# Last experts of a two-layer network: six of eight batches routed to tiles of 256 rows of one expert, two left dense

## The chip, the core and the metric

The kernel runs on one core of one Trainium2 chip. The metric is the time of one execution in device microseconds. The core has TensorE (PE, with its weight loads PEld), VectorE (DVE), ScalarE (ACT), GpSimd (POOL) and the queue engine SyncE (SP). Each works through its own list of instructions in order, and they wait for one another through semaphores. Everything is float32.

## The reference

The input is 8 batches of 512 rows of 256 columns. Two layers are computed, each a mixer and a feed-forward part with experts. Only the second layer's feed-forward part matters here; `x` is the running sum of 4096 rows.

```python
flat = layernorm(x)                                  # rows of 256
scores = sigmoid(flat @ Wg.T)                        # 16 experts
s_choice = scores + bias_corr                        # groups of 4: the sum of the two best of each,
                                                     # the 2 best groups, then the 4 best experts in them
w = scores[chosen]; w = w / (sum(w) + 1e-20) * 2.5
hid = relu(einsum('th,eih->eti', flat, W1)) ** 2     # 16 experts, 256 -> 128
y = einsum('eti,ehi->eth', hid, W2)                  # 128 -> 256
out = einsum('eth,te->th', y, cw)                    # cw holds w for the 4 chosen, else 0
shared = relu(flat @ Ws1.T) ** 2 @ Ws2.T             # 256 -> 256 -> 256, every row
x = x + out + shared
```

## The kernel before

Five stages run one after the other: A and B are layer one's mixer and attention, C layer one's experts (routed through DRAM to 35 tiles of 128 rows, with `L1065` scattering rows and `L1827` gathering them on POOL), D layer two's mixer, and E the experts above. Between stages all engines meet. X holds all 4096 rows in the working memory Z (SBUF) throughout, 32 tiles of 128 x 256; PS is PSUM.

Stage E (class `StageE`) computes all 16 experts for all rows. It goes batch by batch. `order` writes one list of steps, and every engine walks that list and does its part of each step:
- `prep(b, p)`, p = 0 to 17: statistics, normalizing, transposing (PE, L2360), logits (PE, L2367), and choosing by comparing each score with each other (DVE, with POOL's multiply and add). Pieces of batch b + 1 stand between the experts of batch b.
- `hidden(b, j)`: two matmuls (each two records in the trace) of 512 columns (L2384), relu on ACT, and the product on DVE (L2517). j = 0, 1 is the shared expert, 2 to 17 the routed ones.
- `down(b, x, i)`: x = 0 is the shared expert, x = 1 to 16 expert x - 1, i the half of the batch. Matmuls of 256 columns (L2402) into one of four PSUM banks, then DVE adds the result times the row's weight `cw` into X (L2532). A bank is taken again when the addition four units back is done (`e.wait_ge(s["acc"], u - 3)`).

SP loads the weights at the stage's start and stores each batch when its 34 `down` units are added.

## Time and profile before

| | us |
|---|---|
| median of three runs | 3163.64 |
| lowest and highest | 3160.22, 3163.8 |
| the profiled execution's own time | 3162.49 |
| its span, first to last instruction | 3160.6 |
| PE busy in the span | 2702.3 (85%) |
| DVE busy | 2132.8 (67%) |
| ACT busy | 1586.8 (50%) |
| POOL busy | 1181.4 (37%) |
| mean granted TensorE clock, full speed is 1 | 0.933 |

Busy times are of the whole span, over five stages with different limits, so what a change in stage E is worth has to be read from that stage. Times inside the trace count from the span's start. A transfer's landing is counted from its issue.

### The profile page before, as it was taken

Reading aid. Unit: us, or ns where it says so; the run is one execution under the profiler, and the core shown is the slowest. Engines: PE = TensorE matmul, PEld = TensorE weight load, DVE = VectorE, ACT = ScalarE, POOL = GpSimd, SP = SyncE. Lnnn points to the kernel's source line nnn. Section 1 sums busy time; section 2 is a strip of 40 time slices with the busy share of each in tenths; the row PEclk is TensorE's granted clock in tenths of the full one; section 3 lists DMA queues with packets and bytes.
Section 4 is the critical chain, followed back from the end, with each engine's and each line's share of the span. In section 5 each row is a group of like instructions: output and inputs, shape, how many; then the busy total and the mean of one; then the engine's idle time right before and its main releaser. Section 6 shows DMA issues by size and latency. Waiting matters only on the chain.

```text
span 3160.6 us, 39455 instructions
## 1 busy us (share of the span) xinstructions
PE 2702.3 (85%) x13080; PEld 1625.4 (51%) x13142; DVE 2132.8 (67%) x4071; ACT 1586.8 (50%) x2357; POOL 1181.4 (37%) x874
## 2 busy tenths in 40 slices
PE   7778878887765689999886999967989988999999
PEld 4445544454443255555544666644444445666666
DVE  1688889788886777877633222227887876777776
ACT  3678778778872245555541111127787781111111
POOL 0788888888882221111101000024455430100000
PEclk9899999899877799999998999988988999999999
DMA  3578878788784765555605000020000002000000
GB/s 114 114 169 148 180 170 161 155 179 168 150 189 96 195 177 102 81 86 87 96 14 188 24 24 22 19 56 7 8 14 7 8 1 61 7 14 7 7 7 14
DMA packets 122343, 262.88 MB, mean 83 GB/s; under 512 B 14785, under 2 KB 76993, under 8 KB 120481
## 3 DMA queue, kind: packets, MB, share of 16 engines
q0 software_dynamic: 28000, 134.89, 20.9%
q1 hardware_dynamic: 94144, 125.47, 17.3%
q8 instruction: 110, 1.80, 0.2%
q14 instruction: 89, 0.72, 0.1%
HBM read 135.40 MB, written 131.20 MB: 84 GB/s over the span
## 4 chain that ended last, share of the span: by engine, by line
PE 47%; DVE 7%; issue 7%; ACT 3%; POOL 2%; DMA 1%; POOLq 0%; DVEq 0%; ACTq 0%
PE PS L2384 7%; PE PS L1676 6%; PE PS L2402 6%; PE PS L1970 3%; PE PS L1698 3%; PE PS L2014 3%; PE PS L1339 2%; PE PS L2032 2%; PE PS L1297 1%; PE PS L1267 1%; PE PS L1321 1%; PE PS L1318 1%; DVE PS L1527 1%; POOL Z L2229 1%; ACT Z L2100 1%
## 5 line engine op out<-in xcount | busy, mean ns | idle before, releaser
L856 POOL TENSOR_TENSOR Z<-Z 128x1024 f32<-128x1024 f32 x256 | 645.2, 2722 | 123.7 <-DVE Z L757 78.6
L764 DVE TENSOR_TENSOR_SCAN Z<-PS,Z 128x1024 f32<-128x1024 f32 x256 | 576.4, 2274 | 20.7 <-ACT PS L684 10.4
L535 PE MATMUL PS<-Z 128*128 128x128 f32 x2048 | 301.4, 293 | 119.9 <-DVE Z L764 48.2
L535 PEld LDWEIGHTS PS<-Z 128*128 128x128 f32 x2048 | 248.3, 150 | 253.0 <-issue 84.1
L684 ACT ACTIVATE PS<-Z 128x511 f32<-128x511 f32 x512 | 332.8, 688 | 65.0 <-DVE Z L764 63.5
L1527 DVE CUSTOM_DVE_ANT_0 PS<-PS,Z 128x512 f32<-128x512 f32 (+3 forms) x512 | 242.2, 511 | 122.5 <-PE PS L1297 117.4
L1435 ACT ACTIVATE Z<-PS 128x512 f32<-128x512 f32 x320 | 188.7, 596 | 254.8 <-PE PS L1321 251.8
L2435 ACT ACTIVATE Z<-PS 128x512 f32<-128x512 f32 x144 | 85.9, 597 | 411.9 <-PE PS L2384 411.9
L696 ACT ACTIVATE Z<-PS,Z 128x512 f32<-128x512 f32 x378 | 245.9, 684 | 77.2 <-PE PS L535 69.1
L2384 PE MATMUL PS<-Z 128*128 128x512 f32 x576 | 273.5, 600 | 7.9 <-DVE Z L2517 7.1
L2100 ACT ACTIVATE Z<-Z 128x2048 f32<-128x2048 f32 x128 | 249.9, 1994 | 34.1 <-PE PS L2014 21.8
L487 PE MATMUL PS<-Z 128*128 128x512 f32 x512 | 246.6, 611 | 9.7 <-ACT Z L604 9.0
L1676 PE MATMUL PS<-Z 128*128 x560 | 248.3, 596 | 0.6 <-issue 0.4
L2402 PE MATMUL PS<-Z 128*128 128x256 f32 x1024 | 243.0, 380 | 1.8 <-DVE Z L2532 1.8
L2402 PEld LDWEIGHTS PS<-Z 128*128 128x128 f32 x1024 | 193.6, 190 | 80.3 <-issue 53.6
L2532 DVE SCALAR_TENSOR_TENSOR Z<-PS,Z 128x256 f32<-128x256 f32 x512 | 213.9, 476 | 9.9 <-PE PS L2402 9.9
L2517 DVE TENSOR_TENSOR Z<-Z,PS 128x512 f32<-128x512 f32 x144 | 98.3, 686 | 130.7 <-ACT Z L2435 130.6
L1574 POOL TENSOR_TENSOR Z<-Z 128x512 f32<-128x512 f32 x32 | 37.0, 1157 | 390.1 <-ACT Z L1400 390.1
L1803 DVE TENSOR_TENSOR Z<-Z,PS 128x512 f32<-128x512 f32 x70 | 48.2, 689 | 197.6 <-PE PS L1676 197.6
L2014 PE MATMUL PS<-Z 128*32 128x512 f32 x1024 | 138.1, 634 | 42.3 <-DVE Z L2201 42.3
L1676 PEld LDWEIGHTS PS<-Z 128*128 128x128 f32 x560 | 104.5, 192 | 119.6 <-issue 119.6
L2201 DVE TENSOR_SCALAR Z<-Z 128x2048 f32<-128x2048 f32 x128 | 157.4, 1242 | 5.6 <-ACT Z L2100 5.2
(293 smaller groups left out, 4896.5 us busy)
## 6 DMA issues: line engine op xcount, KB each, us to landing
sums<-Z POOLq DMA_DIRECT2D x112, 768.0 KB, 8.2
Z<-rows_b SPq DMA_DIRECT2D x128, 256.0 KB, 4.7
Z<-scr SPq DMA_DIRECT2D x256, 128.0 KB, 5.5
rows_n<-in_L_ffn_expert_wv POOLq DMA_DIRECT2D x32, 528.0 KB, 7.4
scr<-Z SPq DMA_DIRECT2D x32, 384.0 KB
Z<-Z POOLq DMA_DIRECT2D x14, 768.0 KB, 7.3
Z<-in_L_ffn_expert_wv SPq DMA_DIRECT2D x4, 2048.0 KB, 14.7
Z<-sums SPq DMA_DIRECT2D x7, 768.0 KB, 6.4
```

The source lines that it names most:

```text
L487: ins = e.matmul(self.bank("conv", b, c)[0], self.conv[:, w, k, c * 128:(c + 1) * 128], self.n_fm[:, k, w:w + 512], start=i == 0, stop=i == 7)
L535: ins = e.transpose(self.turned[i % 2][:, c * 128:(c + 1) * 128], self.h(k, c // 2)[:, c % 2, i * 128:(i + 1) * 128], ident)
L684: ins = e.activation(self.aa[f][:, c, 1:512], self.de[b % 2][:, 2 * f + c, 1:512], ACT.Exp, scale=self.An[:, q:q + 1])
L696: e.activation(self.pr[k % 3][:, i - 1, :], self.turned[i % 2], ACT.Copy, scale=self.ct[b % 2][:, i, 16 + n:17 + n]).then_inc(s["yprod"], 1)
L764: e.tensor_tensor_scan(h, a, h, 0.0, ALU.mult, ALU.add).then_inc(s["scan"], 1)
L856: e.tensor_tensor(self.h(k, f), self.du[b % 2][:, 2 * f:2 * f + 2, :], b3(self.Bs[k % 2], 1, [128, 2, 512]), ALU.mult).then_inc(s["hin"], 1)
L1527: ins = e.tensor_tensor_reduce(x[:, at:at + w], x[:, at:at + w], self.mask[:, 512 - w:512], -1.0, 3e38, ALU.add, ALU.min, nm[:, i, h8:h8 + 1])
L1676: ins = e.matmul(ub[n], self.hs[c % 2][:, k, :], self.wv[:, bass.ds(expert[c] * 4096 + (2048 * k + 512 * n), 512)], start=k == 0, stop=k == 1)
L2014: ins = e.matmul(self.wb[w % 2][32 * j:32 * j + 32, :], self.wpick[u % 8][:, q, :], self.e[u % 10][:, q, :], start=q == 0, stop=q == 3)
L2100: e.activation(self.e[u % 10], self.An, ACT.Exp, scale=self.dl[b % 2][:, j, i:i + 1]).then_inc(s["grow"], 1)
L2384: ins = e.matmul(self.up[n % 2], w, self.nf[b % 2][:, k, :], start=k == 0, stop=k == 1)
L2402: ins = e.matmul(o[:, j * 256:(j + 1) * 256], self.hd[n % 4][:, c], self.w2[:, x - 1, :], start=True, stop=True)
```

## The change

Batches 0 to 5 (R = 6) are routed; 6 and 7 stay dense. The order of the batches is 0, 1, 2, 6, 3, 4, 5, 7 (`SEQ`), and a preparation of batch k of this order begins at half-step `BEGIN[k]`, so that up to four are under way at a time.

- Preparation: choosing is now done by DVE alone, with its instructions for the eight greatest and their places (`max`, `max_index`) and one-hot masks of 256 columns. ACT normalizes; for a routed batch it writes each row four times, side by side, into `src`. To each of the four copies come its weight (column 256) and the row number in the result to which it belongs (column 257), so a row is 258 words.
- `places`, `spots`: PE counts with a triangular matrix how many earlier rows chose the same expert; DVE makes of it the row in DRAM to which each copy goes. `spread`: POOL scatters them, 16 indirect DMAs of 128 rows for a batch, into `rows_e`, where each expert has a region.
- `table`: after the last routed batch DVE computes how many tiles of 256 rows each expert has and which expert and rows a tile takes. SP fills 256 rows behind each expert's last with empty rows (weight 0, a result row that is not read). Eight more fills stand at the stage's start.
- The tile loop, always 64 tiles (`NQ`): SP loads 256 rows; PE transposes them (`heads`); DVE copies the transposed rows out of PSUM and the expert's first weights to a fixed place; PE multiplies (`ups`), ACT and DVE make the squared relu, PE multiplies with the second weights, whose address comes from a register (`downs`), ACT scales by the row's weight, and POOL scatters the 256 result rows to `rows_z` with two indirect DMAs. PE's `downs` stand three tiles behind.
- Then batch 7 is done densely, and between its steps DVE adds the four results of each routed row (`yadd`), which SP has read back, 2 MB a batch. Squares are now made on ACT for the shared and dense experts.

The shared expert is computed densely for all eight batches as before.

```diff
-    PIECES = 18
...
+    NE, R, CAP, NG = 16, 6, 6 * 512 + 256, 12
+    NQ = 8 * R + 16
+    NS = 2 * NQ
+    ROW = 258
+    SEQ = (0, 1, 2, 6, 3, 4, 5, 7)
+    BEGIN = (0, 2, 4, 6, 10, 16, 22, 28)
+
+    PREP = ((0, ("stats",)), (1, ("rstd",), ("minus",)), (2, ("norm",)), (3, ("flip",), ("flipped",)), (4, ("logits",), ("sig",)),
+            (5, ("choose",)))
+    ROUTED = ((5, ("hidden", 0)), (6, ("places",), ("hidden", 1)), (7, ("spots",), ("spread",), ("down", 0, 0), ("down", 0, 1)))
+    DENSE = ((5, ("hidden", 0)), (6, ("hidden", 1)), (7, ("down", 0, 0), ("down", 0, 1)))
...
+    def dense(self, b):
+
+        out = [("hidden", b, 2), ("hidden", b, 3)]
+        for x in range(16):
+            if x + 4 < 18:
+                out.append(("hidden", b, x + 4))
+            out += [("down", b, x + 1, 0), ("down", b, x + 1, 1)]
+        return out
...
+        first, work = [], self.dense(6)
+        start, last = self.BEGIN[self.SEQ.index(6)] + 8, self.BEGIN[-1] + 8
+        for h in range(last):
+            for k, b in enumerate(self.SEQ):
+                plan = self.PREP + (self.ROUTED if b < self.R else () if b == 7 else self.DENSE)
+                for at, *steps in plan:
+                    if at == h - self.BEGIN[k]:
+                        first += [(s[0], b) + s[1:] for s in steps]
+                        first += [("table",)] * (("spots",) in steps and b == self.R - 1)
+            upto = max(0, h - start) * 50 // (last - start)
+            while 50 - len(work) < upto:
+                first.append(work.pop(0))
+        first += work
+        final = [("hidden", 7, 0), ("hidden", 7, 1), ("down", 7, 0, 0), ("down", 7, 0, 1)]
+        for n, step in enumerate(self.dense(7)):
+            final.append(step)
+            if n % 8 == 6 and n // 8 < self.R:
+                final.append(("yadd", n // 8))
+        return first, final
...
+        for q in range(8):
+            at = 16 * self.CAP + 512 * q
+            e.dma_start(m.rows_e[at:at + 512].rearrange("(a r n) c -> a r (n c)", a=4, r=32),
+                        d["pads"][4 * q:4 * q + 4].rearrange("a (r n) c -> a r (n c)", r=32)).then_inc(s["d_fill"], 16)
+        out = m.out.rearrange("b (i p) c -> b p i c", p=128)
+        e.wait_ge(s["ends"], 1)
+        for x in range(16):
+            at = e.value_load(self.ends[0:1, x:x + 1], min_val=0, max_val=16 * self.CAP - 256)
+            e.dma_start(m.rows_e[bass.ds(at, 256)].rearrange("(h p) c -> h p c", h=2), d["pads"][2 * x:2 * x + 2]).then_inc(s["d_fill"], 16)
+        e.wait_ge(s["slot"], 1)
+        e.wait_ge(s["d_fill"], 16 * 24)
...
+        for q in range(self.NQ):
+            if q >= self.NG:
+                e.wait_ge(*self.scattered(2 * (q - self.NG)))
+                e.wait_ge(*self.scattered(2 * (q - self.NG) + 1))
+            at = e.value_load(self.slot[0:1, 128 + q:129 + q], min_val=0, max_val=16 * self.CAP + 15 * 256)
+            e.dma_start(self.g[:, q % self.NG, :, :], m.rows_e[bass.ds(at, 256)].rearrange("(h p) c -> p h c", p=128)).then_inc(
+                self.d_g[q % self.NG], 16)
+            if q == 3:
+                e.wait_ge(s["acc"], self.u1)
+                e.dma_start(out[6], m.X[:, 24:28, :]).then_inc(m.d_out, 16)
+        for c in range(self.NS - 8, self.NS):
+            e.wait_ge(*self.scattered(c))
+        for b in range(self.R):
+            if b >= 3:
+                e.wait_ge(s["yadd"], b - 2)
+            e.dma_start(self.yb[b % 3], m.rows_z[2048 * b:2048 * (b + 1)].rearrange(
+                "(i p j) c -> p i (j c)", p=128, j=4)).then_inc(self.d_back[b % 3], 16)
+            if b >= 3:
+                e.dma_start(out[b - 3], m.X[:, 4 * b - 12:4 * b - 8, :]).then_inc(m.d_out, 16)
+        for b in range(self.R - 3, self.R):
+            e.wait_ge(s["yadd"], b + 1)
+            e.dma_start(out[b], m.X[:, 4 * b:4 * b + 4, :]).then_inc(m.d_out, 16)
+        e.wait_ge(s["acc"], len(self.dnx))
+        e.dma_start(out[7], m.X[:, 28:32, :]).then_inc(m.d_out, 16)
...
+        def heads(q):
+            if q < 2:
+                e.wait_ge(*ring.done(self.n_ring - 1))
+                e.wait_ge(*ring.done(self.n_ring - 2))
+            else:
+                e.wait_ge(s["hs"], q - 1)
+            e.wait_ge(*self.loaded(q))
+            for h in range(2):
+                for k in range(2):
+                    ins = e.transpose(self.hb[q % 2][:, 256 * k + 128 * h:256 * k + 128 * (h + 1)],
+                                      self.g[:, q % self.NG, h, 128 * k:128 * (k + 1)], ident)
+            ins.then_inc(s["ht"], 1)
+
+        def ups(q):
+            e.wait_ge(s["hs"], q + 1)
+            if q < 3:
+                e.wait_ge(s["relu"], self.n1)
+                e.wait_ge(s["acc"], self.u1)
+            else:
+                e.wait_ge(s["pm"], q - 2)
+            expert[q] = e.value_load(self.slot[0:1, q:q + 1], min_val=0, max_val=15 * 256)
+            for k in range(2):
+                ins = e.matmul(self.ub[q % 3], self.wq[q % 4][:, 128 * k:128 * (k + 1)], self.hs[q % 4][:, 256 * k:256 * (k + 1)],
+                               start=k == 0, stop=k == 1)
+            ins.then_inc(s["pu"], 1)
+
+        def downs(q):
+            e.wait_ge(s["pm"], q + 1)
+            if q >= 3:
+                e.wait_ge(s["py"], q - 2)
+            at = expert.pop(q)
+            for h in range(2):
+                ins = e.matmul(self.db[q % 3][:, 256 * h:256 * (h + 1)], self.hm[q % 4][:, 128 * h:128 * (h + 1)],
+                               self.w2f[:, bass.ds(at, 256)], start=True, stop=True)
+            ins.then_inc(s["pd"], 1)
+
+        self.walk(self.pairs, {"heads": heads, "ups": ups, "downs": downs})
+        self.walk(self.last, {"hidden": hidden, "down": down})
...
+        def ups(q):
+            e.wait_ge(s["pu"], q + 1)
+            e.activation(self.rp[q % 4], self.ub[q % 3], ACT.Relu).then_inc(s["pr"], 1)
...
+        def downs(q):
+            e.wait_ge(s["pd"], q + 1)
+            if q >= 4:
+                for c in (2 * q - 8, 2 * q - 7):
+                    e.wait_ge(*self.scattered(c))
+            for h in range(2):
+                ins = e.activation(self.yo[q % 4][:, 256 * h:256 * (h + 1)], self.db[q % 3][:, 256 * h:256 * (h + 1)], ACT.Copy,
+                                   scale=self.g[:, q % self.NG, h, 256:257])
+            ins.then_inc(s["py"], 1)
...
+        def choose(b):
+            sc, ms, gv, oh, tmp = self.sc, self.ms, self.gv, self.oh, self.tmp
+            scf, gvf = sc.rearrange(FLAT), gv.rearrange(FLAT)
+            e.wait_ge(*ring.done(self.uses["logits", b, 0]))
+            step(e.tensor_scalar(scf, scf, 1.0, None, ALU.add))
+            step(e.reciprocal(scf, scf))
+            step(e.tensor_tensor(ms, sc, b3(self.bias, 1, [128, 4, 16]), ALU.add))
...
+            for i in range(4):
+                ins = e.max(self.v8[:, i, :], ms[:, i, :])
+            step(ins)
+            for i in range(4):
+                ins = e.max_index(self.ix8[:, i, :], self.v8[:, i, :], ms[:, i, :])
+            step(ins)
+            step(e.tensor_copy(self.ixf, self.ix8[:, :, 0:4]))
+            step(e.tensor_tensor(oh, b3(self.ixf.rearrange(FLAT), 2, [128, 16, 16]), b3(self.iota, 1, [128, 16, 16]), ALU.is_equal))
+            oh4, tmp4 = (x.rearrange("p (i j) e -> p i j e", j=4) for x in (oh, tmp))
+            step(e.tensor_tensor(tmp4, oh4, sc.unsqueeze(2).to_broadcast([128, 4, 4, 16]), ALU.mult))
+            if b < R:
+                step(e.tensor_reduce(self.pick, oh.rearrange("p (i j) e -> p i e j", j=4), AX.X, ALU.add))
+                e.tensor_copy(self.ohb, self.pick).then_inc(s["ob"], 1)
+            step(e.tensor_reduce(self.wj.rearrange(FLAT), tmp, AX.X, ALU.add))
...
+        def spots(b):
+            r = self.uses["places", b, 0]
+            o = ring.buf(r)
+            e.wait_ge(s["prod"], r + 1)
+            step(e.tensor_tensor(self.a, o[:, 0:64].rearrange("p (i e) -> p i e", e=16), b3(self.run, 1, [128, 4, 16]), ALU.add))
+            e.tensor_tensor(self.run, self.run, o[:, 64:80], ALU.add).then_inc(*ring.over(r))
+            oh4, tmp4 = (x.rearrange("p (i j) e -> p i j e", j=4) for x in (self.oh, self.tmp))
+            step(e.tensor_tensor(tmp4, oh4, self.a.unsqueeze(2).to_broadcast([128, 4, 4, 16]), ALU.mult))
+            step(e.tensor_reduce(self.spotf, self.tmp, AX.X, ALU.add))
+            e.tensor_copy(self.spot[b % 3], self.spotf).then_inc(s["spot"], 1)
...
+        def heads(q):
+            e.wait_ge(s["ht"], q + 1)
+            if q >= 4:
+                e.wait_ge(s["pu"], q - 3)
+            e.tensor_copy(self.hs[q % 4], self.hb[q % 2])
+            at = e.value_load(self.slot[0:1, q:q + 1], min_val=0, max_val=15 * 256)
+            e.tensor_copy(self.wq[q % 4], self.w1f[:, bass.ds(at, 256)]).then_inc(s["hs"], 1)
+
+        def ups(q):
+            e.wait_ge(s["pr"], q + 1)
+            if q >= 4:
+                e.wait_ge(s["pd"], q - 3)
+            e.tensor_tensor(self.hm[q % 4], self.rp[q % 4], self.ub[q % 3], ALU.mult).then_inc(s["pm"], 1)
+
+        def yadd(b):
+            e.wait_ge(self.d_back[b % 3], 16 * (b // 3 + 1))
+            xx = m.X[:, 4 * b:4 * b + 4, :]
+            for j in range(4):
+                ins = e.tensor_tensor(xx, xx, self.yb[b % 3][:, :, 256 * j:256 * (j + 1)], ALU.add)
+                if j < 3:
+                    step(ins)
+            ins.then_inc(s["yadd"], 1)
+
+        self.walk(self.first, {"stats": stats, "minus": minus, "choose": choose, "spots": spots, "table": table, "down": down})
...
+        def spread(b):
+            if b >= 3:
+                e.wait_ge(self.d_spread[b % 3], 256 * (b // 3))
+            e.tensor_copy(self.srci[b % 3][:, :, :, 257], self.dest[:, 16 * b:16 * (b + 1)].rearrange("p (i j) -> p i j", j=4)).then_inc(
+                *own.tick())
+            e.wait_ge(*own.now())
+            e.wait_ge(s["chosen"], self.k(b) + 1)
+            e.wait_ge(s["spot"], b + 1)
+            for t in range(16):
+                e.indirect_dma_start(m.rows_e, bass.IndirectOffsetOnAxis(ap=self.spot[b % 3][:, t:t + 1], axis=0),
+                                     self.src[b % 3][:, t // 4, t % 4, :], None).then_inc(self.d_spread[b % 3], 16)
+
+        def downs(q):
+            e.wait_ge(s["py"], q + 1)
+            for c in (2 * q, 2 * q + 1):
+                if c >= 8:
+                    e.wait_ge(*self.scattered(c - 8))
+                e.indirect_dma_start(m.rows_z, bass.IndirectOffsetOnAxis(ap=self.gi[:, q % self.NG, c % 2, 257:258], axis=0),
+                                     self.yo[q % 4][:, 256 * (c % 2):256 * (c % 2 + 1)], None).then_inc(self.d_y[c % 8], 16)
+
+        self.walk(self.first, {"spread": spread})
+        self.walk(self.pairs, {"downs": downs})
```

How the engines' lists stand. On PE, in stage E, from the middle of one batch of the kernel before; L2360 is the transposing, L2384 and L2402 the two matmuls of dense experts:

```order
L2360 MATMUL PS<-Z 128x128 x8
L2384 MATMUL PS<-Z 128x512 x2
L2402 MATMUL PS<-Z 128x256 x4
L2384 MATMUL PS<-Z 128x512 x2
L2402 MATMUL PS<-Z 128x256 x2
L2367 MATMUL PS<-Z 128x16 x8
L2402 MATMUL PS<-Z 128x256 x2
```

and one tile of the tile loop after the change, where L2575 is `heads`, L2588 `ups` and L2598 `downs` of three tiles earlier, and TENSOR_LOAD and ISA read and check a register:

```order
L2575 MATMUL PS<-Z 128x128 x4
L2586 TENSOR_LOAD Z
L2586 ISA x2
L2588 MATMUL PS<-Z 128x256 x2
L2598 ISA
L2598 MATMUL PS<-Z 128x256 x2
```

For a tile PE has 8 listed matmuls of 128 and 256 columns in the place of 512-column ones. On DVE, the end of stage E before:

```order
L2517 TENSOR_TENSOR Z<-Z,PS 128x512
L2532 SCALAR_TENSOR_TENSOR Z<-PS,Z 128x256 x4
L2517 TENSOR_TENSOR Z<-Z,PS 128x512
L2532 SCALAR_TENSOR_TENSOR Z<-PS,Z 128x256 x4
L2517 TENSOR_TENSOR Z<-Z,PS 128x512
L2532 SCALAR_TENSOR_TENSOR Z<-PS,Z 128x256 x8
```

and one tile of the loop after (L2799 and L2801 are `heads`, L2807 is `ups`):

```order
L2799 COPY Z<-PS 128x512
L2800 TENSOR_LOAD Z
L2800 ISA x2
L2801 ISA
L2801 COPY Z<-Z 128x256
L2807 TENSOR_TENSOR Z<-Z,PS 128x256
```

and DVE's last instructions of the stage, batch 7 with the sums of 1024 columns (L2813, `yadd`):

```order
L2813 TENSOR_TENSOR Z<-Z 128x1024 x4
L2791 SCALAR_TENSOR_TENSOR Z<-PS,Z 128x256 x12
L2813 TENSOR_TENSOR Z<-Z 128x1024 x4
L2791 SCALAR_TENSOR_TENSOR Z<-PS,Z 128x256 x10
L2813 TENSOR_TENSOR Z<-Z 128x1024 x4
L2791 SCALAR_TENSOR_TENSOR Z<-PS,Z 128x256 x10
L2813 TENSOR_TENSOR Z<-Z 128x1024 x4
L2791 SCALAR_TENSOR_TENSOR Z<-PS,Z 128x256 x14
L2813 TENSOR_TENSOR Z<-Z 128x1024 x4
```

The sums are new in DVE's list between the additions of the dense experts. On POOL, the end of the stage before, one batch's choosing:

```order
L2548 TENSOR_TENSOR Z<-Z 128x16 x6
L2553 TENSOR_TENSOR Z<-Z 128x64
L2556 TENSOR_TENSOR Z<-Z 128x64
L2553 TENSOR_TENSOR Z<-Z 128x1024
L2556 TENSOR_TENSOR Z<-Z 128x1024
```

and after the change, the last two batches' `spread` and the tile loop's scatters:

```order
L2829 COPY Z<-Z 128x16
L2835 DMA rows_e<-Z 57344x258 x16
L2829 COPY Z<-Z 128x16
L2835 DMA rows_e<-Z 57344x258 x16
L2843 DMA rows_z<-Z 16384x256 x128
```

POOL's arithmetic is gone; 96 scatters of 258 columns and 128 of 256 stand in its place.

## Rows read from the trace of the kernel before

**Rows 1.** Busy time by stretch: window, length, busy by engine, clock, DMA share, GB/s
```profile
2612.20:2700.00 87.80, 77.81 (x272) 50.37 (x272) 59.00 (x151) 16.47 (x31) 12.18 (x20) 0.92 0.19 55
2700.00:3160.60 460.60, 449.35 (x1648) 299.81 (x1648) 329.29 (x786) 83.21 (x155) 36.56 (x60) 1.00 0.03 10
...
1900.00:2000.00 100.00, 100.00 (x373) 62.48 (x372) 25.97 (x46) 19.31 (x36) 8.52 (x9) 1.00 0.08 24
```

**Rows 2.** Chain of waits in stage E: start, us, what
```profile
2757.09 1.73 PE PS L2384 x4
...
2782.50 1.03 PE PS L2360 x8
...
2789.56 1.69 PE PS L2367 x16
...
2821.47 1.73 PE PS L2402 x8
2823.20 1.73 PE PS L2384 x4
```

**Rows 3.** Timeline, first 30 us of stage E: start, us, engine, line
```profile
2612.23 1.41 DVE L192 BATCH_NORM_STATS2 Z<-Z 128x6 f32<-128x256 f32 x4
...
2618.85 3.75 PE L2384 MATMUL PS<-Z 128*128 128x512 f32 x4 [0.73 <-issue]
...
2622.40 1.93 PE L2367 MATMUL PS<-Z 128*128 128x16 f32 x16
...
2624.92 0.55 DVE L2462 RECIPROCAL Z<-Z 128x64 f32<-128x64 f32 x1
...
2639.16 0.22 DVE L2498 TENSOR_TENSOR Z<-Z 128x64 f32<-128x64 f32 x1
2639.42 0.22 DVE L2500 TENSOR_REDUCE Z<-Z 128x4 f32<-128x64 f32 x1
```

**Rows 4.** Timeline around the start of stage C, with POOL's indirect DMAs
```profile
1638.14 0.96 POOL L1065 DMA_INDIRECT rows_n<-Z  x1 [0.30 <-issue]
...
1684.44 1.00 POOL L1827 DMA_INDIRECT Z<-rows_n,Z  x1 [5.40 <-DMA rows_n<-Z]
...
1690.06 0.50 PEld L1676 LDWEIGHTS PS<-Z 128*128 128x128 f32 x2 [0.84 <-issue]
```

**Rows 5.** Timeline at the end of stage E
```profile
3153.29 0.69 DVE L2517 TENSOR_TENSOR Z<-Z,PS 128x512 f32<-128x512 f32 x1 [1.19 <-ACT Z L2435]
...
3157.14 0.37 SPq L2340 DMA_DIRECT2D out<-Z  x1
```

**Rows 6.** Groups of stage C: busy us, mean ns, idle before
```profile
L1812 DVE COPY Z<-PS 128x512 f32<-128x512 f32 x31 | 21.4, 691 | 86.6 <-PE PS L1687 86.5
...
L1730 ACT ACTIVATE Z<-PS 128x256 f32<-128x256 f32 x30 | 11.6, 385 | 143.8 <-PE PS L1698 143.8
```

**Rows 7.** Timeline of stage D, indirect DMAs beside DVE
```profile
2101.60 1.53 POOL L2229 DMA_INDIRECT Z<-rows_y,Z  x1 [0.30 <-issue]
...
2163.23 0.81 DVE L2143 TENSOR_SCALAR Z<-Z 128x512 f32<-128x512 f32 x1 [2.57 <-ACT Z L2052]
...
2168.53 2.06 POOL L2229 DMA_INDIRECT Z<-rows_y,Z  x1 [0.30 <-issue]
...
2169.08 0.48 DVE L2143 TENSOR_SCALAR Z<-Z 128x512 f32<-128x512 f32 x1
```

**Rows 8.** Single lines: duration min/median/max ns; issue to landing us
```profile
L1550 DVE TENSOR_TENSOR Z<-PS,Z x32: 424/424/425, 1121.1 to 1650.8; 128x256 f32<-128x256 f32 x32
...
L1806 DVE TENSOR_TENSOR Z<-Z x8: 1218/1218/1218, 1731.5 to 2051.2; 128x1024 f32<-128x1024 f32 x8
...
L1636 SPq DMA_DIRECT2D Z<-in_L_ffn_expert_wv x4: 396/470/630, 1659.4 to 1660.9; - x4
...
DMA to landing us min/median/max: 7.9/14.7/22.6
...
DMA to landing us min/median/max: 2.7/2.7/6.4
```

479 lines of the change are left out of this document (280 added, 199 removed).

## The prediction

> **What bounds the kernel now.** I read the page's first line for the span, then busy time by stretch, the chain of waits, and the timeline and single lines where a price was wanted. The last stage runs from 2612.2 to 3160.6 us, 548.4 us of the span of 3160.6. In it PE is busy 527 us, at a granted clock of 0.92 in the first 88 us and 1.00 after; DVE is busy 388, ACT 100, POOL 49 [rows 1]. The chain of waits returns to the same step 66.11 us later (2757.09, 2823.20) [rows 2]. One expert of one batch is 4 matmul records of 512 columns in 1.73 us and 8 of 256 in 1.73 us: 3.44 us, sixteen times, and the shared expert another 6.9; transposing is 1.03 and the logits are 1.69 [rows 2]. That makes 62 + 3 of the 66.1 us. So PE's matmuls bound the stage and every other engine has room: taking matmuls away pays until another engine binds. Nothing before the last stage is touched.
>
> **What is removed.** The 16 routed experts of six batches done densely: 6 x 16 x 3.44 = 330 us of PE. They stay for batches 6 and 7. With them go the ranking on POOL and the 1024-wide compares on DVE.
>
> **What is added** falls into three stretches, since each waits for the one before.
>
> *1. Preparation, dense batch 6, spreading.* The half-steps hold, on PE: 8 x (1.03 + 1.69) = 22 us, shared experts of seven batches 7 x 6.9 = 48, dense experts of batch 6 16 x 3.44 = 55, and counting, 6 matmuls a batch at 0.11 us (1.69 / 16), with weights about 4: 129 us. DVE: choosing is 33 instructions. A 64-wide one is 0.22 and the next starts 0.26 later, a reciprocal is 0.55 [rows 3]; four are 256 wide, between 0.22 and the 0.69 of 512 [rows 5], I take 0.40. Together 28 x 0.24 + 0.55 + 1.6 = 8.9 us, eight times 71. Statistics 8 x 1.8 (1.41 [rows 3] and the aggregation), spots 6 x 1.5, shared additions 14 x 0.69, dense ones 64 x 0.43, the table 4: 137 us. POOL: 96 scatters, each 0.96 us and 0.30 us to the next [rows 4]: 96 x 1.26 = 121 us. ACT passes 256 columns in 0.39 us [rows 6]; 24 norms four times as wide at about 1.1 and some 60 passes of 512 at about 0.6 are 65 us, not the bound.
> Three engines with 121 to 137 us do not overlap perfectly. Up to half-step 14 PE waits for DVE: 12 us from the start to batch 0's logits (they began 10 us into the stage before, at 2622.40 [rows 3], and the norm is now wider), then four choices (36), three spots (4.5), additions and statistics (11): about 64 us. PE is cold there: four records of 512 columns took 3.75 us at the stage's start against 1.73 later [rows 2, 3], the 1.2 GHz level; this lies beside DVE's choosing. From 14 to 29 PE is behind: three preparations with shared experts at 10.3 us, and 34 of the 50 dense steps at 1.1 us, are 68, and I add 7, because DVE chooses in one piece of 8.9 us and PE's four result banks cover 6.9 of it. Half-step 29 is near 139. Then three things run side by side. POOL's last 16 scatters are 20 us and their landing 5.4 (so long POOL waited behind the last scatter [rows 4]). PE's other 16 dense steps and batch 7's transposes are 25 us with the wait for the table. SP has 16 fills of 264 KB behind the counts: an issue is 0.37 us [rows 5], and the register load before it has no row. It is bounded below by nothing and above by the 0.84 us that PE's weight loading stood idle in stage 3 before its first matmul behind such a load [rows 4]; that is 0.4 to 1.2 for both, I take 1.4 with the bounds checks, 22 us, and 4 for landing. The first tile load is another 3 to 4 us (a gather of rows landed after 2.7 [rows 8]). So tiles begin at about 170 us; bounds 155 (perfect overlap) and 190.
>
> *2. 64 tiles of 256 rows.* The 64 run whatever the counts are. Per tile PE has 4 transposes at 0.13 and 8 matmul records of 256 columns at 0.216: 2.25 us [rows 2]. Stage 3's loop, which also takes a weight address from a register, kept PE at 100.00 of 100 us [rows 1], so such loads need not gap PE. ACT: one relu and two scaled copies of 256 columns at 0.39: 1.2. DVE: the copy of 512 from PSUM 0.69 [rows 6], a 256-wide copy of weights about 0.28 (0.48 is a 512-wide instruction [rows 7]), the square 0.42 [rows 8]: 1.4, and with a register load of 0.84 at most 2.24. SP: one load per tile, 1.4. POOL: two scatters, 2 x 1.26 = 2.53. **POOL is the bound**, just ahead of PE. DMA: 528 KB per tile; stage 3 moved the same 1 KB rows at 24 GB/s for a share of 0.08 [rows 1], so 300 GB/s full and 1.8 us per tile.
> POOL's price may grow. An indirect DMA of stage 4 took 1.53 us, but 2.06 with a single-input DVE instruction of 0.48 us inside it; and that DVE instruction, started inside a running one, took 0.81 [rows 7]. They exclude each other. The weight copy is one such meeting per tile, worth 0 to 0.28; I take 0.12. A tile is 2.65, 64 are 170 us, bounds 162 and 180; plus 7 us for the first tile to pass through.
> The Trainium skill's page "SBUF — State Buffer", section "SBUF: two separate sides", says that such a copy locks GpSimd out of writing descriptors until it ends, and that the block lasted about 115 ns beyond. By that rule each tile pays the whole copy and those 115 ns: an estimate of 2.92 us per tile, 187 us, and 3044 us for the kernel. The rows show the mechanism, not that every tile meets it.
>
> *3. Dense batch 7 and the sums.* PE is about 4 us ahead of POOL's end, then has 62 us. Beside it DVE has 29 us of additions and six sums of 4 x 1.22 us [rows 8] = 4.9. Each holds DVE up, but PE's four banks cover 6.9 us: hidden. Read back are 6 x 2 MB; four loads of 2 MB issued within 1.5 us landed after 7.9 to 22.6 us [rows 8], 8.4 MB in 24 us, 6 us each: not the bound, and the first lands about 17 us into the stretch, where DVE asks for it. The last sum stands 4 dense steps before the end, so DVE ends 4 us behind PE instead of 1. Then the store: issue at 3157.14 [rows 5], end at 3160.6, 3.5 us. So 62 + 4 + 4 = 70.
>
> **Sum.** 170 + 7 + 170 - 4 + 70 = 413 us against 548.4, 135 less. 2612.2 + 413 = 3025 of span; the profiled execution ran 1.9 us over its span (3162.49): 3027. The median of before, 3163.64, is 1.2 above that execution, so nothing is corrected. A difference under 0.2% (6 us) could not be told from none.
>
> **Rivals.**
> *POOL binds at 2.65 us per tile*: 3027. For it: the constant 0.96 + 0.30. Chance 0.49.
> *The tile loop hangs on another hand-over*: the register load on DVE or SP costs 1 to 2 us. DVE at 1.4 + 1.6 to 1.4 + 2.1 is 3.0 to 3.5 us per tile, 22 to 54 us more: 3049 to 3081, middle 3065. For it: no row prices that load, and DVE waits for PE, for ACT and for itself in one queue. Against it: PE in stage 3. Chance 0.28.
> *Less waiting in the first stretch, and no meeting of copy and scatter*: 155 and 162: 3004. Against it: DVE's choosing in one piece. Chance 0.13.
> *The clock*: PE is busy 2.25 of 2.65 us. Were every tile at the lower level, its records would cost double, 4.5 us per tile, 118 more: 3145. Against it: the clock stood at 1.00 wherever PE hardly stopped [rows 1]. Chance 0.04.
> *Slower than before*: scattered rows land late. A result buffer is refilled when the scatter four tiles back has landed, so a tile is at least (issue 2.5 + landing + ACT 1.2) / 4. This binds from a landing of 6.9 us on and reaches the old time at 4.8 us per tile, a landing of 15.5 us. The one row is the 5.4 us wait [rows 4], with few other transfers. At 20 us: 5.9 per tile, 208 more, 3235. Chance 0.06, of which 0.02 falls near the old time.
>
> The range: 2990 lies below the lower bounds of the stretches together (3004) by what the last stretch may still save; 3085 takes in the hand-over rival. Outside are the clock, the late landing and some of the ends: about 0.15. Faster 0.49 + 0.28 + 0.13 + 0.04 = 0.94.
>
> **What would show it.** Right: a steady tile period near 2.6 us with POOL's scatters back to back 0.30 apart, PE and DVE waiting; the first scatter about 25 us after the stage's start; tiles from about 170; sums that no matmul waits for. Wrong: POOL idle between tiles (with DVE, SP or a landing named), scatters well above 1 us, a granted clock well under 1 in the tiles, or SP's fills ending long after the last scatter landed.

## The result and the profile after

The changed kernel took 3084.41 us (median of 4, 3082.6 to 3087.08) against 3161.93 for the kernel before, run beside it: ratio 0.9756, 95% interval 0.9739 to 0.9773. Predicted were 3027 us in 2990 to 3085. The direction was right and the time lies at the very edge of the range: 77.5 us came off, not 135. The gain does not hold everywhere: on another occasion, on chip D below, the same program took 3180.99 us, 1.0061 times the kernel before (run x9_again).

Busy time by stretch in the changed kernel. The four rows are what I had called stretch 1, the first tile's way, the tiles and the end (columns as in [rows 1]).

```profile
core 0: us, PE busy (x) PEld busy (x) DVE busy (x) ACT busy (x) POOL busy (x), PEclk, DMA share, GB/s
2617.20:2846.00 228.80, 165.40 (x598) 111.84 (x598) 121.18 (x497) 83.04 (x133) 94.14 (x102) 0.79 0.36 119
2846.00:2855.60 9.60, 8.17 (x45) 6.59 (x46) 6.66 (x15) 2.39 (x6) 0.00 (x1) 1.00 0.87 241
2855.60:3017.70 162.10, 148.45 (x741) 119.52 (x740) 83.71 (x177) 76.80 (x190) 123.35 (x128) 0.98 0.63 191
3017.70:3085.30 67.60, 55.82 (x194) 36.12 (x192) 54.99 (x89) 19.70 (x32) 0.01 (x1) 0.94 0.67 243
```

The stage took 468 us where it took 548 [rows 1]; it also began 5 us later (2617.2, not 2612.2), and stage starts in later traces spread over 2603 to 2623, so below each is measured from its own. 229 + 10 + 162 + 68 us stand against my 170 + 7 + 170 - 4 + 70. The tiles and the end came out within 8 us; the first stretch took 59 us more.

The second view is the one line of POOL's result scatters (minimum, median, maximum in ns; then the first and last start).

```profile
L2843 POOL DMA_INDIRECT rows_z<-Z x128: 957/963/1037, 2855.6 to 3016.7; - x128
```

127 intervals in 161.1 us are 1.27 us each, 2.54 a tile: a scatter of 0.96 and 0.30 to the next, as [rows 4] had them, and hardly anything more.

The waits of the first stretch name what went wrong (engine and line, for whom; us in total, times, longest):

```profile
ACT Z L2647 <- PE PS L2543: 106.9, 27, 10.7
POOL rows_e L2835 <- DVE Z L2754: 83.5, 5, 34.1
DVE Z L2791 <- PE PS L2558: 39.8, 15, 9.9
...
PE PS L2517 <- DVE Z L2732: 30.4, 6, 7.9
```

POOL waits for DVE's spots (L2754), DVE for PE's downs (L2558), PE for DVE's choosing (L2732), ACT for PE: each engine waits for another, and none is busy throughout. The timeline shows one turn, PE first, then DVE:

```profile
2635.92 1.10 PE L2495 MATMUL PS<-Z 128*128 128x128 f32 x8 [1.57 <-ACT Z L2626]
2644.32 0.21 PE L2517 MATMUL PS<-Z 128*128 128x64 bf16 x1 [7.30 <-DVE Z L2732]
...
2644.54 3.45 PE L2543 MATMUL PS<-Z 128*128 128x512 f32 x4
2647.82 1.85 PE L2507 MATMUL PS<-Z 128*128 128x16 f32 x16
2649.53 3.70 PE L2558 MATMUL PS<-Z 128*128 128x256 f32 x16
```

```profile
2635.90 1.41 DVE L194 BATCH_NORM_STATS2 Z<-Z 128x6 f32<-128x256 f32 x4 [8.01 <-ACT Z L2626]
...
2637.64 0.17 DVE L2703 TENSOR_SCALAR Z<-Z 128x64 f32<-128x64 f32 x1
...
2654.50 1.41 DVE L194 BATCH_NORM_STATS2 Z<-Z 128x6 f32<-128x256 f32 x4 [8.88 <-ACT Z L2626]
2655.94 0.38 DVE L198 BATCH_NORM_AGGREGATE Z<-Z 128x2 f32<-128x6 f32 x4
2656.23 0.20 DVE L2749 TENSOR_TENSOR Z<-PS,Z 128x64 f32<-128x64 f32 x1
```

The counts of batch 0 (L2517) were ready near 2644.8, but DVE read them (L2749) at 2656.23, since the statistics of batch 6 stood ahead in its list and waited for ACT's norm of batch 2. In ACT's list that norm stood behind the exponential of batch 1's logits. PE made those logits only behind a hidden step, which took it 3.45 us at the lower clock level (1.73 in [rows 2]). Choosing itself took 7.9 us (my 8.9).

### The profile page after: what moved, and what is told of

Its sections match the earlier page's. It is cut to its first block, busy times and chain, and to the rows that moved or that the text cites. A ratio compares the mean times of both kernels' runs of the same rounds, so it can differ in the third digit from the quotient of the medians.

```text
span 3085.3 us, 39824 instructions
## 1 busy us (share of the span) xinstructions
PE 2554.8 (83%) x12734; PEld 1552.1 (50%) x12796; DVE 2009.3 (65%) x3911; ACT 1671.0 (54%) x2533; POOL 1351.2 (44%) x1024
## 4 chain that ended last, share of the span: by engine, by line
PE 39%; issue 8%; DVE 8%; ACT 5%; POOL 4%; DMA 3%; SPq 0%; POOLq 0%; DVEq 0%; ACTq 0%
PE PS L1678 6%; PE PS L1972 3%; PE PS L1700 3%; PE PS L2016 3%; PE PS L2543 2%; PE PS L2558 2%; PE PS L1341 2%; POOL rows_z L2843 2%; PE PS L2034 2%; PE PS L1269 1%; PE PS L1299 1%; DMA rows_z<-Z 1%; PE PS L1323 1%; PE PS L1320 1%; DVE PS L1529 1%
## 5 line engine op out<-in xcount | busy, mean ns | idle before, releaser
L537 PEld LDWEIGHTS PS<-Z 128*128 128x128 f32 x2048 | 250.9, 151 | 256.2 <-issue 85.9
L1437 ACT ACTIVATE Z<-PS 128x512 f32<-128x512 f32 x320 | 188.9, 597 | 253.7 <-PE PS L1323 250.7
L489 PE MATMUL PS<-Z 128*128 128x512 f32 x512 | 246.2, 610 | 10.0 <-ACT Z L606 9.3
L1805 DVE TENSOR_TENSOR Z<-Z,PS 128x512 f32<-128x512 f32 x70 | 48.2, 689 | 197.5 <-PE PS L1678 197.5
L2254 POOL TENSOR_TENSOR Z<-Z 128x128 f32<-128x128 f32 x128 | 81.7, 748 | 209.2 <-PE PS L2016 202.9
L1829 POOL DMA_INDIRECT Z<-rows_n,Z x35 | 33.2, 950 | 304.9 <-PE PS L1666 298.3
L1678 PEld LDWEIGHTS PS<-Z 128*128 128x128 f32 x560 | 104.4, 192 | 119.5 <-issue 119.5
L2843 POOL DMA_INDIRECT rows_z<-Z x128 | 123.4, 964 | 64.8 <-issue 29.9
L1320 PE MATMUL PS<-Z 128*128 128x384 bf16 (+3 forms) x482 | 144.1, 299 | 8.5 <-ACT Z L1437 6.4
L1323 PE MATMUL PS<-Z 96*128 96x384 bf16 (+3 forms) x512 | 150.2, 305 | 0.0
L2835 POOL DMA_INDIRECT rows_e<-Z x96 | 92.8, 967 | 111.2 <-DVE Z L2754 83.5
```

Source lines behind the costliest of these rows:

```text
L489: ins = e.matmul(self.bank("conv", b, c)[0], self.conv[:, w, k, c * 128:(c + 1) * 128], self.n_fm[:, k, w:w + 512], start=i == 0, stop=i == 7)
L537: ins = e.transpose(self.turned[i % 2][:, c * 128:(c + 1) * 128], self.h(k, c // 2)[:, c % 2, i * 128:(i + 1) * 128], ident)
L1437: e.activation(self.pt[n % 8], self.tbank[n % 2], ACT.Exp).then_inc(s["exp"], 1)
L1678: ins = e.matmul(ub[n], self.hs[c % 2][:, k, :], self.wv[:, bass.ds(expert[c] * 4096 + (2048 * k + 512 * n), 512)], start=k == 0, stop=k == 1)
L2843: e.indirect_dma_start(m.rows_z, bass.IndirectOffsetOnAxis(ap=self.gi[:, q % self.NG, c % 2, 257:258], axis=0), self.yo[q % 4][:, 256 * (c ...
```

## The experiments

In the table "first", "tiles" and "end" are us from the stage's start to the first result scatter, from there to the last one's start, and to the end of the span. These come from the one profiled execution of each run, while the median is over all of its executions. Chips are lettered. Which chip A is isn't on record, so it may be one of the others. The runs of one letter were all made on one occasion. A ratio is to the kernel before, run beside it, its medians being 3165.2 on B, 3169.4 on C, 3165.7 on D, 3161.6 on E. The unaltered changed kernel ran on A and D only, so the differences of x1 to x4 below are between B and A.

| run | chip | first | tiles | end | median | ratio (95%) |
|---|---|---|---|---|---|---|
| changed kernel | A | 238.4 | 161.1 | 68.6 | 3084.4 | 0.9756 (.9739-.9773) |
| x1_alone | B | 271.9 | 161.5 | 68.6 | 3114.8 | 0.9843 (.9827-.9859) |
| x2_once | B | 226.5 | 161.3 | 69.2 | 3067.0 | 0.9681 (.9632-.9730) |
| x3_lists | B | 196.3 | 160.8 | 69.4 | 3036.4 | 0.9598 (.9581-.9615) |
| x4_dense | B | 209.5 | 160.6 | 69.7 | 3052.2 | 0.9647 (.9629-.9665) |
| x5_three | C | 260.7 | 198.0 | 77.3 | 3143.1 | 0.9899 (.9867-.9932) |
| x6_half | C | 286.4 | 133.0 | 73.4 | 3112.6 | 0.9812 (.9777-.9848) |
| x7_split | C | 293.8 | 198.0 | 83.5 | 3190.5 | 1.0059 (1.0036-1.0082) |
| x8_ahead | C | 287.5 | 204.4 | 67.5 | 3181.5 | 1.0027 (1.0009-1.0046) |
| x9_again | D | 291.4 | 197.8 | 70.7 | 3181.0 | 1.0061 (1.0042-1.0080) |
| x10_four | D | 257.4 | 201.9 | 67.4 | 3145.9 | 0.9946 (.9929-.9964) |
| x11_paced | E | 214.8 | 199.4 | 67.8 | 3088.2 | 0.9768 (.9738-.9798) |
| x12_four_again | E | 254.9 | 199.9 | 67.9 | 3138.6 | 0.9921 (.9895-.9947) |

**x1_alone**

```diff
-    BEGIN = (0, 2, 4, 6, 10, 16, 22, 28)
+    BEGIN = (0, 8, 16, 24, 32, 40, 48, 56)
```

> Undoes one part of the change: the eight preparations begin 8 half-steps apart (0, 8, 16, ... 56), so that one is under way at a time; everything else stays as changed. My theory (the first stretch is a chain in which TensorE, VectorE and ScalarE take turns because each engine works its list strictly in order): a batch alone costs its whole chain, about 1.8 of statistics, 0.7 of ScalarE's root, 4.6 of fourfold normalising, 1.5 to 2 of transposes, 1.1 of copies, 3.5 of logits, 7.9 of choosing, 1.5 to 2 of places and spots, about 24 us, and the shared expert's downs behind it at the lower clock 5 to 10 more, so about 30 a batch against the 21 seen with several under way; the first results are then scattered about 20 to 50 us later than the 238 us after the stage's start that the changed kernel took, and the kernel takes 3105 to 3135 us. Rival (each engine's own sum of work sets the stretch, as I predicted it): with the same sums of work the start of the tiles moves by under 10 us, 3080 to 3095 us.

First results came 33.5 us later, the rest as before. The engines' work is the same, so their sums don't set this stretch; the chains do. (PE's granted clock in the first 88 us was 0.61, against 0.69, so a part of the loss is its colder steps.)

**x2_once**

```diff
-                    o, x = self.src[b % 3][:, i, :, 0:256], b3(x, 1, [128, 4, 256])
+                o = self.src[b % 3][:, i, 0, 0:256] if b < self.R else self.nt[:, i, :]
...
+        def copies(b):
+                    ins = e.activation(self.src[b % 3][:, i, 1:4, 0:256], b3(self.src[b % 3][:, i, 0, 0:256], 1, [128, 3, 256]), ACT.Copy)
```

`copies` is a new step behind `sig`; `spread` waits for it.

> ScalarE normalises each routed batch once (256 wide, as it does for batch 6 in 2.07 us) and signals; the other three copies of a row are made from the first behind the logits' exponential, where only the spreading waits for them. The rival that ScalarE's fourfold normalising (4.64 us, 11.1% of the chain of waits between 2611 and 2860) is what stretches the first part: 2.6 us a batch come off the chain, in five or six batches, 13 to 15 us, 3068 to 3073 us. My theory (the order of the lists, with the choosing behind the downs and the statistics behind the next batch's normalising): the statistics of the next batch wait less, but the copies stand ahead of the shared expert's squares on ScalarE, so the two nearly cancel, 3075 to 3087 us.

The profiled execution had 11.9 us less in the first stretch. ACT's fourfold norm is part of the chain, as that rival said, but a small one of the 59. The size is rough: the four executions lay between 3046.1 and 3079.0 us.

**x3_lists**

```diff
-    PREP = ((0, ("stats",)), (1, ("rstd",), ("minus",)), (2, ("norm",)), ...
+    PREP = ((1, ("stats",), ("rstd",)), (2, ("minus",), ("norm",)), ...
-    ROUTED = (..., (6, ("places",), ("hidden", 1)), (7, ("spots",), ("spread",), ("down", 0, 0), ("down", 0, 1)))
+    ROUTED = (..., (6, ("hidden", 1)), (7, ("places",), ("spots",), ("spread",)), (8, ("down", 0, 0), ("down", 0, 1)))
```

> The same work, begun in the same half-steps, but four kinds of step stand at another place of the lists: the statistics one half-step later (behind a choosing, no longer ahead of it), the places one half-step later and right ahead of the spots, the shared expert's downs one half-step later (behind the next choosing). Theory of the turns: VectorE no longer waits for TensorE's downs ahead of a choosing nor for ScalarE's normalising ahead of the spots, so a batch costs VectorE's own 1.9 + 7.9 + 1.5 + 1.3 plus small waits, 14 to 17 us in place of 21 in the first four, and 5 to 10 less in the others; the tiles begin 25 to 40 us earlier, 3045 to 3060 us. Rival, TensorE's lower clock alone: its work is the same and the stretch shrinks by under 8 us, 3077 to 3085 us. Rival, the order of the lists does not matter since the chain of one batch is as long as ever: 3084 us.

42.1 us came off the first stretch, a little more than expected, with no work removed. Where steps stand in the lists is the largest cause that was found. POOL's wait for the spots fell from 83.5 us to this (us in total, five times as before, the longest):

```profile
POOL rows_e L2835 <- DVE Z L2754: 36.7, 5, 19.4
```

The granted clock of the first 88 us rose from 0.69 to 0.84 with no edit for it, while PE was busy 64.79 us of them and not 54.41. So the 42 us include what the clock gave back. Changed kernel, then x3:

```profile
2617.20:2705.00 87.80, 54.41 (x195) 37.99 (x196) 43.22 (x206) 33.86 (x55) 35.76 (x40) 0.69 0.47 157
```

```profile
2604.40:2692.20 87.80, 64.79 (x284) 45.74 (x285) 60.04 (x274) 46.05 (x74) 46.94 (x51) 0.84 0.52 175
```

**x4_dense**

```diff
-    SEQ = (0, 1, 2, 6, 3, 4, 5, 7)
+    SEQ = (6, 0, 1, 2, 3, 4, 5, 7)
```

What was done once at batch 0 (the wait for the weights, DVE's constants) is now done at batch 6.

> Batch 6, one of the two that run all 16 experts densely, is prepared first (batches in the order 6, 0, 1, 2, 3, 4, 5, 7), so its 50 expert steps are spread from half-step 8 and not from half-step 14; batch 0 begins one place later. It tests the share of the clock and of TensorE's idle time: the granted clock, 0.69 in the first 88 us and 0.85 in the next 100, should be at or above 0.85 and 0.95. Rival of the clock: the 1.7 to 2 us that a warm batch of downs, logits or hiddens saves come off the chain and the tiles begin 10 to 20 us earlier, 3062 to 3075 us. Theory of the turns: the dense steps stand ahead of the places in TensorE's list and VectorE's choosing stands behind their additions, so what the clock gives is mostly taken by more work between the turns, and the later half-steps, which hold fewer dense steps, give some back: 3070 to 3090 us.

28.9 us came off, more than either theory gave. The clock in the first 88 us and the next 100 was 0.79 and 0.95, against 0.69 and 0.83; 0.85 had been expected for the first. The gain can't be split into clock and idle time filled.

**x5_three**: the edits of x2, x3 and x4 together.

> The three edits of the first part together: the lists of the third experiment, one normalised copy ahead of the transposes and three behind the logits, and batch 6 first. In stage E they took 41.6, 11.1 and 28.3 us off alone. If each took away a different wait they add up to 81 us, which is more than is there: the work of VectorE alone in this stretch was summed to 137 us, and 25 to 31 more pass from the last spread to the first scatter of results, so the first results can't be scattered before about 165 us after the stage's start against 196 in the third experiment. I expect that the lists leave the other two half of what they gave, 10 to 20 us: first results at 176 to 186 us, 3016 to 3028 us for the kernel. Rival: the three all cut the same waits and 3030 to 3036 us stay.

It missed both: first results at 260.7 us, later than the changed kernel's, and tiles 37 us longer although nothing in them was edited. x9_again below shows that the edits are not to blame.

**x6_half**: of POOL's loop over a tile's two scatters one is left. Half of the expert outputs reach no row, and the sums at the end read rows of the earlier layer in their place.

> The second of each tile's two scatters of results is left out (half of the expert outputs reach no row), and the sums at the end read the same number of rows from the expert outputs of the earlier layer, which are all written. Everything else, PE's work and the loads among it, is as in the changed kernel. Theory (GpSimd, with 0.96 us and 0.30 us beside it for each scatter, sets the 2.54 us of a tile): the period falls to what TensorE needs, 0.94 busy of 2.54 or about 2.39 us, at most to 2.25, so the 64 tiles take 144 to 153 us in place of 162 and the kernel 9 to 18 us less, 3066 to 3075 us. Rival (GpSimd only keeps step with a loop that something else limits, the meeting of the register load and the weight copy on VectorE or the landing of results before ScalarE may write again): the period stays within 0.03 us, 3080 to 3086 us.

Its time is no guide, since the first stretch had x5's trouble. But the loop answers: 63 intervals in 133.0 us are 2.11 us a tile. That is shorter than the 2.54 of POOL's two scatters on A and the 3.1 on C (x5 and x7, 198 us for 64), and PE is now never idle. This is its stretch of tiles:

```profile
2903.30:3037.20 133.90, 133.90 (x725) 116.00 (x723) 79.81 (x175) 77.30 (x188) 61.54 (x64) 1.00 0.62 169
```

So the scatters did set the tile, on A by POOL's own 2.54 us, and PE would come next at 2.11 (I had 2.25).

**x7_split**: batches 1, 3 and 5 are summed by the same four additions on GpSimd behind its scatters, with a semaphore of their own.

> The sums of batches 1, 3 and 5 at the end go from VectorE (5.0 us for a batch's four additions) to GpSimd, which has nothing to do behind its last scatter; its addition of 128x1024 took 2.72 us in the first stage, 10.9 for a batch. Theory (behind the tiles VectorE, with 29.4 us of sums and 25.9 of dense additions, has a backlog and ends 6 us behind TensorE): the end comes about 2 us behind TensorE's last product plus the store, 4 to 7 us earlier, 3077 to 3081 us. Rival (the transfers of the batches' rows, which land 7.5 to 16.8 us from their issue, set the end): no change, 3083 to 3086 us. Rival (both engines add in the same memory and hinder each other, VectorE's additions become longer than 1.22 us): 3086 to 3095 us.

The end took 83.5 us, 6 more than in x5 on that chip. It took 15 more than the changed kernel's, but a part of that is a wait for ACT that x5 has too (see x8). The third theory, that the two engines hinder each other, was right. The additions of the sums at the end of x7, on POOL and DVE (count, busy us, mean ns of one):

```profile
L2856 POOL TENSOR_TENSOR Z<-Z 128x1024 f32<-128x1024 f32 x12 | 28.6, 2380 | 40.9 <-DMA Z<-rows_z 40.2
...
L2819 DVE TENSOR_TENSOR Z<-Z 128x1024 f32<-128x1024 f32 x12 | 24.8, 2066 | 0.3
```

DVE's 12 additions took 2.07 us each, not 1.22: together 24.8 us, in place of 29.4 for all 24. Hardly anything was taken off DVE, and POOL's three sums waited 40.2 us for their rows. The first sums of both, POOL and DVE, show how they share:

```profile
3119.39 10.12 POOL L2856 TENSOR_TENSOR Z<-Z 128x1024 f32<-128x1024 f32 x4 [15.97 <-DMA Z<-rows_z]
```

```profile
3123.51 8.35 DVE L2819 TENSOR_TENSOR Z<-Z 128x1024 f32<-128x1024 f32 x4
```

From the first's start to the last's end are 12.47 us. One after another, at POOL's median of 2.00 and DVE's 1.22, the eight would take 12.9. The Trainium skill, page "SBUF — State Buffer", section "SBUF: two separate sides", has this as an exclusive lock on the port pair that the two engines share: when DVE's instruction has two inputs in SBUF and GpSimd's reads SBUF, whichever starts first holds it for its whole instruction. The trace agrees, with 12.47 us against 12.9.

**x8_ahead**

```diff
-        self.walk(self.pairs, {"ups": ups, "downs": downs})
-        self.walk(self.last, {"hidden": hidden})
+        self.walk(self.pairs[:-3], {"ups": ups, "downs": downs})
+        self.walk(self.last[:2], {"hidden": hidden})
+        self.walk(self.pairs[-3:], {"downs": downs})
+        self.walk(self.last[2:], {"hidden": hidden})
```

> ScalarE takes the first two hidden tiles of batch 7 ahead of the last three tiles' scalings in its list; in the changed kernel they stood behind them, and TensorE waited 5.4 us for them at the end of the tiles. Theory (the end stretch starts when TensorE may go on with batch 7): 3 to 5 us less, 3079 to 3082 us. Rival (VectorE's backlog and the rows' transfers, which can't start before the last scatter, set the end anyway): within 1 us of 3084.

Nothing can be said from its time. The end took 67.5 us, and 67.4 to 67.9 in x10, x11 and x12, which have the edit too, against 68.6 and 70.7 in the two runs of the changed kernel: about 1 to 3 us. It gives more where PE waits longer: in x5 PE waited 10.5 us for ACT at this place and the end took 77.3 us; x10, the same kernel with this edit, took 67.4.

**x9_again**: the changed kernel, unaltered.

> The changed kernel itself, unaltered, once more. The last four kernels had, in identical code ahead of their edits, stretches of 4 to 28 us in which ScalarE and VectorE waited for a signal of TensorE that had been due, all of them while GpSimd's scatters were under way; their first results came 260.7 to 293.8 us after the stage's start, against 238.4 in the changed kernel and 196 to 272 in the four before. Theory (it is the chip that they ran on, which passes on the engines' signals late while scatters complete, and no property of their edits): the changed kernel has the same late signals when it runs on such a chip and then takes 3170 to 3190 us; on one like those of the first experiments it takes 3078 to 3092 us with no such wait. Rival (the four edits brought the waits, by the placement of code or semaphores): 3080 to 3090 us and no late signal on any chip.

It took 3180.99 us, so the four edits did not bring the trouble. The program is the same as on A; what differs is the occasion and, as far as is known, the chip. No chip is known to have run it twice, so the two can't be told apart, and "chip" below stands for both. One place shows what happens. PE ended batch 1's downs (L2558) at 2659.36 + 6.54 = 2665.90 and the next hidden step (L2543) at 2667.61. These are PE, DVE and ACT in x9:

```profile
2659.36 6.54 PE L2558 MATMUL PS<-Z 128*128 128x256 f32 x16
2665.73 1.88 PE L2543 MATMUL PS<-Z 128*128 128x512 f32 x4
2667.45 1.03 PE L2495 MATMUL PS<-Z 128*128 128x128 f32 x8
2697.57 0.21 PE L2517 MATMUL PS<-Z 128*128 128x64 bf16 x1 [29.08 <-DVE Z L2732]
```

```profile
2677.64 0.69 DVE L2784 TENSOR_TENSOR Z<-Z,PS 128x512 f32<-128x512 f32 x1 [22.54 <-DMA Z<-in_L_ffn_expert_proj]
2690.26 0.69 DVE L2784 TENSOR_TENSOR Z<-Z,PS 128x512 f32<-128x512 f32 x1 [11.93 <-DMA Z<-in_L_ffn_expert_proj]
```

```profile
2690.31 0.60 ACT L2647 ACTIVATE Z<-PS 128x512 f32<-128x512 f32 x1 [23.16 <-remote]
```

DVE's second addition began 24.4 us after the downs had ended, ACT's relu 22.7 us after its matmuls, and the two began within 0.05 us of each other. On chip A the same downs ended at 2672.76 + 6.41 = 2679.17, and DVE's second addition began 0.04 us later:

```profile
2679.21 0.69 DVE L2784 TENSOR_TENSOR Z<-Z,PS 128x512 f32<-128x512 f32 x1 [1.96 <-PE PS L2558]
```

The releaser that is named in x9 ("remote", a weight load of stage C) is one that nobody waits for here. Records of semaphore events are missing in the traces of C, D and E (x9 has the landing of none of its 224 scatters), and then the name is not to be trusted; the row that PE ended is. The long waits with such names all end inside POOL's runs of scatters or within 5 us behind one (this run went from 2645.1 to 2685.7), none later in the gaps between. It is not PE's signals alone. Inside a later run DVE waited 4.4 us for the signal of its own step before, which costs it next to nothing on A (us in total, times, longest):

```profile
DVE Z L2726 <- issue: 4.4, 1, 4.4
```

The kernel before takes the same on all the chips (3162 to 3169). The missing records and the late signals come in the same traces, so a part of the recording in the lateness is not excluded; no run here tests it.

**x10_four**: x5 and the edit of x8.

> The three edits of the first part together (the lists of the third experiment, one normalised copy ahead of the transposes and three behind the logits, batch 6 first), and ScalarE's first two hidden tiles of batch 7 ahead of the last three tiles' scalings. On a chip without the late signals: the first results at 176 to 190 us after the stage's start, the tiles 161 us, the end 64 to 68 us, 3010 to 3035 us in all. On a chip with them: first results at 255 to 265 us as in the fifth experiment, tiles 198 us, end 67 us or more, 3130 to 3145 us. Rival of the three edits' sum (they cut the same waits): no earlier than the third experiment's 196 us, 3030 to 3036 us without late signals.

The stretches are as expected for such a chip, within 4 us: 257.4, 201.9 and 67.4 us, and the time, 3145.9, is 1 us above its range. Even there the edits are worth 35 us against x9 on the same chip.

**x11_paced**

```diff
                 e.indirect_dma_start(m.rows_e, ..., self.src[b % 3][:, t // 4, t % 4, :], None).then_inc(self.d_spread[b % 3], 16)
+                e.memset(self.idle, 0.0).then_inc(*own.tick())
+                e.wait_ge(*own.now())
```

To x10's kernel it adds a small fill behind each scatter of `spread`, and a wait for it; `idle` is a new buffer that nothing reads.

> The kernel with the four edits, and one small fill of GpSimd's own memory behind each scatter of the spreading, which does nothing but keep the scatters apart: about 1.6 to 1.7 us from one to the next in place of 1.27. On the chips with late signals, the tiles' scatters came 1.56 us apart on average and the signals were late; with every second scatter left out they came 2.11 us apart and no signal was late. Theory (such a chip completes a scatter in about 1.5 us, and a signal waits behind the completions that have piled up): on such a chip the late waits of the first part mostly go, the first results come at 205 to 230 us after the stage's start in place of 257, and the kernel takes 3095 to 3125 us against 3137 to 3153. Rival (the lateness comes with any scatter under way, whatever its distance to the next): the bursts are longer and the first results later than 257 us, 3145 to 3170 us. On a chip without late signals the fill only makes GpSimd's 16 scatters of a batch 5 to 7 us longer, and the kernel 0 to 25 us slower than its twin without it.

**x12_four_again**: its twin without the fill, on the same chip.

> The kernel with the four edits once more, as the twin of the paced one on its chip. With late signals: 3137 to 3153 us and first results at about 257 us, as before. On a chip without them, where the four edits together have not yet run: the three edits of the first part took 41.6, 11.1 and 28.3 us off singly, of which I expect 50 to 65 us together, and the fourth up to 5 us; first results at 176 to 190 us after the stage's start, 3010 to 3035 us in all. Rival (the three cut the same waits): 196 us and 3030 to 3036 us.

The fill made POOL slower and the kernel 50 us faster. POOL's rows in x11:

```profile
2654.64 0.33 POOL L2846 MEMSET Z<- 128x256 f32 x1
2655.25 0.96 POOL L2844 DMA_INDIRECT rows_e<-Z  x1 [0.28 <-POOL Z L2846]
2656.82 0.96 POOL L2844 DMA_INDIRECT rows_e<-Z  x1 [0.28 <-POOL Z L2846]
```

The scatters are 1.57 us apart, and POOL waits for the spots once, before its first scatter; in x12 it was six times. First x11, then x12:

```profile
POOL rows_e L2844 <- DVE Z L2762: 34.7, 1, 34.7
```

```profile
POOL rows_e L2843 <- DVE Z L2761: 86.8, 6, 35.2
```

Up to the first results the longest wait of ACT or DVE with no releaser named is 6.4 us in x11. x12 has six of ACT and eight of DVE with a wrong releaser, 109 us together, the longest 14.6. First results came 40 us earlier. So the lateness does not come with any scatter under way, as the rival had it: 1.27 us apart they bring it, at 1.57 and 2.11 hardly. That fits signals that pile up behind scatters which complete more slowly than they are issued, but it isn't shown: how long a completion takes was not measured, and the fill also makes POOL wait for a signal of its own behind each scatter, which no run tests apart from the distance. The tile loop, where nothing paces, comes to 1.56 us a scatter by its stalls (198 us / 127), which would fit a completion of about that time.

## Why the prediction was right or wrong

The direction and the two later stretches came from the mechanism that was forecast. That the time fell inside the range was luck: the first stretch went 39 us past its upper bound of 190, and 3085 held only because the range had been widened for the hand-over rival, which did not happen.

- **Stretch 1, 170 us: mis-sized; 229.** The failed step is "three engines with 121 to 137 us do not overlap perfectly", with its allowance of 33 us and bounds of 155 to 190. The sums were not far off: DVE was busy 121 us to my 137, POOL's 96 scatters at 1.27 us are my 121. PE was busy 165 to my 129, but at a granted clock of 0.79; I had laid its cold time beside DVE's choosing. In fact PE, DVE and ACT took turns: PE's cold steps stood between two choosings. I took only the part up to half-step 14 for a chain, let PE's sum stand for the rest, and never walked the lists for what stands ahead of what. x3 shows that 42 of the 59 us hang on the places of four kinds of step, the clock's rise with it included; x1 shows that it is a chain.
- The first scatter was to come 25 us after the start. It came after 41.3 (2658.53), by the wait for the statistics and the norm shown above.
- Of what I ran side by side at the stretch's end, SP's fills (20.3 us for 16) ended 2.7 us behind POOL's last spread, as said. But PE ended last, not SP: SP issued the first tile load at 2837.28, loads landed after 2.6 to 3.8 us, and PE ended batch 6's last downs at 2844.16, 3.07 us of it a wait for DVE behind batch 7's choosing.
- **Stretch 2, POOL binds at 2.65 us a tile: right, 2.54.** The meeting of scatter and weight copy, for which I took 0.12, cost the scatters next to nothing. 44 of the 64 copies (median 297 ns) began inside a scatter and 14 scatters began inside a copy, and still the scatters' median was 963 ns and the longest 1037; the longest copy took 529. The rule of the Trainium skill's page "SBUF — State Buffer", section "SBUF: two separate sides", gave an estimate of 2.92 us a tile; the trace does not agree here.
- **The rival of the register load: wrong.** On DVE its register step took 57 ns, and POOL's scatters stayed back to back:

```profile
L2801 DVEq FUSED_REGOPS  x64: 57/57/65, 2845.5 to 2994.9; - x64
```

  3084 lies next to that rival's 3049 to 3081, but not by its mechanism.
- **Stretch 3, -4 + 70: right, 67.6.** My "DVE ends 4 us behind PE" was 6.6: from 3028.33 on DVE had a sum or additions, with one pause of 0.24 us, until 3080.95, and PE's last product ended at 3074.33. I had no wait at PE's start; it stood 5.4 us behind ACT's list.
- **The rival of the clock: no.** The granted clock in the tiles was 0.98.
- **Slower than before**: I gave it 0.06 and a late landing as its mechanism. On chip D it did come true, 1.0061 (x7 and x8 on C, with edits, took 1.0059 and 1.0027). The trace points to another mechanism, which I did not have: late signals. The tile was 3.1 us there (198 us for 64), and the first results came 53 us later. No landing is recorded in x9, but ACT's scalings, which wait for PE and for the landings, waited 46 us in the tiles, against 61 on A, while its relus, which wait for PE alone, waited 79 against 19.

Open: whether the chip or the occasion brings the late signals, why they come while scatters are under way, and whether what counts is the scatters' number, their packets or their updates. No run had the four edits on a chip like A or B, so their sum there isn't measured (x3 alone reached 3036.4); nor did one pace them there.
